# First cross attention of a fused transformer block: maximum's pieces in threes on 32-row tiles, products and banks reordered

## What is computed

```python
qc = x @ w_q + b_q
kc = y @ w_k + b_k
vc = y @ w_v + b_v
scores = jnp.einsum('bhqd,bhkd->bhqk', qh, kh) / math.sqrt(D_HEAD)
attn = jax.nn.softmax(scores, axis=-1)
out = jnp.einsum('bhqk,bhkd->bhqd', attn, vh)
```

## Time and profile before

| | us |
|---|---|
| median of 3 runs | 1087.43 (1084.34 to 1089.31) |
| profiled execution | 1088.43 |
| its span | 1086.5 |

### The profile page before, as it was taken

The page is one execution under the profiler, slowest core; times in us unless marked ns, Lnnn a source line. Parts: engine busy times, 40 slices in busy tenths (PEclk is TensorE's granted clock), DMA queues, the critical chain, the costliest instruction groups (busy, mean ns, idle before and its releaser), DMA issues. The chain is left out here.

```text
span 1086.5 us, 31222 instructions
## 1 busy us (share of the span) xinstructions
PE 999.8 (92%) x11876; PEld 723.2 (67%) x11876; DVE 718.8 (66%) x1369; ACT 560.7 (52%) x1107; POOL 413.5 (38%) x290
## 2 busy tenths in 40 slices
PE   6857989999999999888779999999999999999997
PEld 3633666666666667646327777777777777777786
DVE  6647767677777777212786767767677677767752
ACT  3623767676776666532444454444454453444542
POOL 6513222232222323020106554545556444555542
PEclk9966999999999999989799999999999999999998
DMA  3416565666566652110020112111011111102100
GB/s 126 122 35 161 161 161 157 177 178 174 169 176 166 174 162 72 50 52 1 2 72 28 58 58 60 52 41 56 21 58 56 58 43 49 43 34 58 36 4 3
DMA packets 90924, 91.34 MB, mean 84 GB/s; under 512 B 50882, under 2 KB 77716, under 8 KB 90868
## 3 DMA queue, kind: packets, MB, share of 16 engines
q1 hardware_dynamic: 90868, 90.56, 29.9%
HBM read 51.15 MB, written 22.18 MB: 68 GB/s over the span
## 5 line engine op out<-in xcount | busy, mean ns | idle before, releaser
L1430 ACT ACTIVATE P<-PS 125x448 f32<-125x448 f32 x384 | 207.1, 544 | 265.8 <-PE PS L1339 263.9
L1320 POOL TENSOR_TENSOR Pl<-P 125x896 f16<-125x896 f32 x128 | 229.9, 1801 | 237.7 <-ACT P L1430 237.7
L1066 DVE TENSOR_REDUCE m<-PS 128x1 f32<-128x500 f32 x336 | 220.8, 675 | 115.4 <-PE PS L1057 113.4
L974 DVE TENSOR_REDUCE m_part<-PS 128x1 f32<-128x500 f32 x336 | 208.1, 673 | 86.5 <-PE PS L878 85.2
L1355 PE MATMUL PS<-cNh,P 125*128 125x97 f16 x1344 | 197.9, 208 | 0.1
L952 ACT ACTIVATE Pb<-PS 125x448 f32<-125x448 f32 x384 | 184.2, 546 | 26.5 <-PE PS L853 24.2
L1357 PE MATMUL PS<-cNh,Pl 125*128 125x97 f16 x1344 | 197.4, 207 | 0.0
L1356 PE MATMUL PS<-cNl,P 125*128 125x96 f16 x1344 | 196.8, 206 | 0.0
L1356 PEld LDWEIGHTS PS<-cNl,P 125*128 125x128 bf16 x1344 | 131.8, 98 | 25.5
L878 PE MATMUL PS<-KH,Qmx 128*128 128x500 f16 x336 | 128.0, 391 | 21.3 <-DVE m_part L974 10.8
L1355 PEld LDWEIGHTS PS<-cNh,P 125*128 125x128 bf16 x1344 | 131.1, 98 | 15.7 <-issue 3.2
(11 more groups left out here) (174 smaller groups left out, 1447.8 us busy)
## 6 DMA issues: line engine op xcount, KB each, us to landing
Kst<-k_halves SPq DMA_DIRECT2D x144, 125.0 KB, 2.7
k_halves<-KH SPq DMA_DIRECT2D x16, 750.0 KB, 3.2
cx<-in_ctx SPq DMA_DIRECT2D x16, 562.5 KB
d_cx<-in_ctx SPq DMA_DIRECT2D x16, 562.5 KB
c_halves<-cHi SPq DMA_DIRECT2D x16, 288.0 KB, 2.9
c_halves<-cLo SPq DMA_DIRECT2D x16, 288.0 KB, 6.5
cTh<-c_halves SPq DMA_DIRECT2D x16, 288.0 KB, 3.1
cTl<-c_halves SPq DMA_DIRECT2D x16, 288.0 KB, 3.9
```

The costliest lines, as they stand in the source:

```text
L974: nc.vector.tensor_reduce(m_part[:, t, part:part + 1], PS[:, 6 + k % 2, 0:SP], AX.X, ALU.max).then_inc(s_reduced, 1)
L1066: nc.vector.tensor_reduce(m21[:, t, part:part + 1], PS[:, S1[k % 2], 0:SP], AX.X, ALU.max).then_inc(n_red, 1)
L1320: nc.gpsimd.tensor_tensor(Pl[:, c % NP], P1[:, c % NP], high, ALU.subtract).then_inc(n_low_p, 1)
L1430: nc.scalar.activation(P1[:, c % NP, half * HALF:(half + 1) * HALF], PS[0:KC, u % 3, 0:HALF], ACT.Exp).then_inc(n_exp, 1)
```

## The change

All is in the first cross attention.

- The maximum's pieces: 24 in place of 21, each a matmul with 32 rows (the four heads of group g) and 112 query columns against 500 keys, without the other heads' zero rows. Three of them with three different g are a "three"; they fill banks 5, 6 and 7, and one reduction of 112 x (3 x 500) takes the maximum. There are 8 threes per sequence. A three starts when the reduction of the one before is done.
- Order: threes 1 to 7 at c = 0, 2, 3, 4, 6, 7, 8; three 0 of the following sequence already at c = 13 of the body before. Values' products at c = 0, 1, 2, keys' products at c = 3, 5, 7, `turn_output` at 8, `turn_attention` at 10, and the four small steps (`highest`) at c = 9.
- Banks: the products, the turns and the maximum's turn share one work bank, 3. `turn_output` therefore waits for the third `split_keys`.
- Transposing DMAs of b + 3: issued in the body of b, between the laying of part 1 and of part 2 of the keys, not at the start of the next body.
- The maximum lies in 8 tiles of 112 queries, so on 16 extra rows of Kst and Qst and not 14, with one more block of columns in the table. The second cross attention keeps its 21 pieces under the name NPC1.

Left out of the diff: those sizes in other lines, and lines where only a bank's name changes.

```diff
-        Kst = sb_in(cross, "Kst", [96 + MR, 2, G, SK], F16)
+        Kst = sb_in(cross, "Kst", [96 + MR0, 2, G, SK], F16)
...
-        m_part = sb_in(cross, "m_part", [128, QT, NSP])
-        mtop = sb_in(cross, "mtop", [128, QT])
-        mhigh = sb_in(cross, "mhigh", [128, QT], F16)
-        mneg = sb_in(cross, "mneg", [128, MR])
+        m_part = sb_in(cross, "m_part", [TP, NSP * G, 2])
+        mtop = sb_in(cross, "mtop", [TP, QT0])
+        mhigh = sb_in(cross, "mhigh", [TP, QT0], F16)
+        mneg = sb_in(cross, "mneg", [TP, MR0])
...
-        OB, WB, WB2, MB = 4, 5, 3, 7
-        K_BANK, V_BANK = (WB2, WB, WB2), WB2
-        V_AT = {7: 0, 9: 1, 12: 2}
...
-        PIECES = [(t, part) for part in range(NSP) for t in range(QT)]
-        NPC = len(PIECES)
-        BESIDE = [range(min(2 * c, NPC), min(2 * c + 2, NPC)) for c in range(NC + LAG0)]
+        OB, WB, SB0 = 4, 3, 5
+        V_AT = {0: 0, 1: 1, 2: 2}
...
+        NPC = 2 * NSP * G // 3
+        K_AT = {3: 0, 5: 1, 7: 2}
+        AFTER_SCORES = {2: 2, 3: 3, 6: 5, 7: 6}
+        AT_END = {0: 1, 4: 4, 8: 7}
+        START = {0: 0, 1: 1, 2: 2, 3: 3, 4: 4, 6: 5, 7: 6, 8: 7}
+        NEXT = {13: 0}
...
+        def three(k):
...
+            return k % 2, range(3 * (k // 2), 3 * (k // 2) + 3)
...
-                    if part == 2 and block_row == 1:
+                    if part == 1 and block_row == 1:
...
-                    if part == 2 and block_row == 2 and inside(i, par, 3):
+                    if part == 1 and block_row == 2 and inside(i, par, 3):
...
+                if part == 1 and turn_next:
+                    turn_rows(sp, i, par, 3)
...
-        def work_bank(banks, k, mode):
+        def work_bank(k, mode):
...
-            return (4, 5, 2)[k] if mode == BESIDE_Q else banks[k]
+            return (4, 5, 2)[k] if mode == BESIDE_Q else WB
         def turn_context(pe, i, par, k, mode):
...
             for c in range(4):
-                mm = pe.transpose(PS[0:DC, work_bank(None, k, mode), c * KC:(c + 1) * KC], cx[:, slot, 4 * k + c, :], ident[0:KC, 0:KC])
+                mm = pe.transpose(PS[0:DC, work_bank(k, mode), c * KC:(c + 1) * KC], cx[:, slot, 4 * k + c, :], ident[0:KC, 0:KC])
...
         def k_piece(pe, i, par, k, mode=LOOP):
...
-                pe.wait_ge(v_kept, (n - 1) * 3)
-            elif k == 1:
-                wait_for(pe, att_kept, n - 3)
+                pe.wait_ge(v_kept, n * 3)
...
-                pe.wait_ge(k_split, n * 3 + 1)
-            o = PS[:, work_bank(K_BANK, k, mode), 0:SP].rearrange("p (c k) -> p c k", c=4)
+                pe.wait_ge(k_split, n * 3 + k)
+            o = PS[:, work_bank(k, mode), 0:SP].rearrange("p (c k) -> p c k", c=4)
...
-                if inside(i, par, 2) and not early:
-                    pe.wait_ge(k_split, n * 3 + 6)
+                if not early:
+                    pe.wait_ge(k_split, n * 3 + 3)
...
             for c in range(4):
-                o = PS[0:KC, V_BANK, c * D:(c + 1) * D]
+                o = PS[0:KC, WB, c * D:(c + 1) * D]
...
             def _(sp):
                 def body(i, par):
-                    if inside(i, par, 2) and not (isinstance(i, int) and i < 0):
-                        turn_rows(sp, i, par, 2)
...
-                        lay_keys(sp, i, par, 2)
+                        lay_keys(sp, i, par, 2, turn_next=inside(i, par, 3))
...
-                def score_piece(i, par, k):
...
-                    slot, n = (par + 1) % 2, i * 2 + par + 1
-                    t, part = PIECES[k]
+                def score_three(i, par, k, ahead):
...
+                    slot, n = (par + ahead) % 2, i * 2 + par + ahead
+                    j, where = three(k)
...
-                    if t == 0:
-                        pe.wait_ge(k_high, n * 3 + part + 1)
-                    wait_for(pe, s_reduced, n * NPC + k - 1)
-                    pe.matmul(PS[:, 6 + k % 2, 0:SP], Qmx[:, slot, t * 128:(t + 1) * 128],
-                              KH[:, slot, 0, part * SP:(part + 1) * SP], start=True, stop=True).then_inc(s_filled, 1)
...
-                def turn_output(n, k_before):
+                    if j == 0:
+                        pe.wait_ge(k_high, n * 3 + where[-1] // G + 1)
+                    wait_for(pe, s_reduced, n * NPC + k)
+                    for at, e in enumerate(where):
+                        part, g = e // G, e % G
+                        rows_of = slice(32 * g, 32 * g + 32)
+                        mm = pe.matmul(PS[0:TP, SB0 + at, 0:SP], Qmx[rows_of, slot, (2 * g + j) * TP:(2 * g + j + 1) * TP],
+                                       KH[rows_of, slot, 0, part * SP:(part + 1) * SP], start=True, stop=True)
+                    mm.then_inc(s_filled, 1)
...
+                def turn_output(n, has_2):
...
-                    if k_before is not None:
-                        pe.wait_ge(k_split, k_before)
+                    if has_2:
+                        pe.wait_ge(k_split, n * 3 + 12)
+                    elif n + 2 < B:
+                        pe.wait_ge(v_kept, n * 3 + 9)
...
-                def turn_maximum(i, par):
+                def turn_maximum(i, par, has_b, has_old):
...
+                    if has_old:
+                        pe.wait_ge(att_kept, n - 1)
+                    else:
+                        pe.wait_ge(k_split, n * 3 + 6)
...
-                    pe.matmul(PS[96:96 + MR, MB, 0:128], mneg[:], ident, start=True, stop=True).then_inc(m_turned, 1)
+                    pe.matmul(PS[96:96 + MR0, WB, 0:TP], mneg[:], ident[0:TP, 0:TP], start=True, stop=True).then_inc(m_turned, 1)
                 def body(i, par):
...
                     for c in range(NC + LAG0):
-                        pieces = list(BESIDE[c]) if has_1 else []
...
-                        for k in pieces[:1]:
-                            score_piece(i, par, k)
+                        if has_1 and c == 11:
+                            turn_maximum(i, par, has_b, has_old)
+                        if has_1 and not at_start and c in AFTER_SCORES:
+                            score_three(i, par, AFTER_SCORES[c], 1)
...
-                        if has_2 and 3 <= c < 6:
-                            k_piece(pe, i, par, c - 3)
-                        if has_b and has_old and c == 6:
-                            turn_output(b - 1, b * 3 + 8 if has_2 else None)
...
+                        if has_2 and c in K_AT:
+                            k_piece(pe, i, par, K_AT[c])
...
+                            turn_output(b - 1, has_2)
+                        if has_b and has_old and c == 10:
...
-                        if has_1 and c == 11:
-                            turn_maximum(i, par)
-                        for k in pieces[1:]:
-                            score_piece(i, par, k)
+                        if has_1 and not at_start and c in AT_END:
+                            score_three(i, par, AT_END[c], 1)
+                        if at_start and c in START:
+                            score_three(i, par, START[c], 1)
+                        if has_2 and c in NEXT:
+                            score_three(i, par, NEXT[c], 2)
...
-                turn_output(B - 1, None)
+                turn_output(B - 1, False)
...
-                        if has_2 and 3 <= c < 6:
-                            keep_keys(act, i, par, c - 3)
-                        if has_b and has_old and c == 8:
-                            keep_attention(b - 1)
...
+                        if has_2 and c in K_AT:
+                            keep_keys(act, i, par, K_AT[c])
+                        if has_b and has_old and c == 10:
+                            keep_attention(b - 1)
...
             def _(dve):
-                def reduce_piece(i, par, k):
-                    n = i * 2 + par + 1
+                def reduce_three(i, par, k, ahead):
+                    n = i * 2 + par + ahead
...
-                    t, part = PIECES[k]
-                    nc.vector.tensor_reduce(m_part[:, t, part:part + 1], PS[:, 6 + k % 2, 0:SP], AX.X, ALU.max).then_inc(s_reduced, 1)
+                    j, where = three(k)
+                    nc.vector.tensor_reduce(m_part[:, where[0]:where[-1] + 1, j], PS[0:TP, SB0:SB0 + 3, 0:SP], AX.X, ALU.max).then_inc(s_reduced, 1)
                 def normalise(n):
...
+                def highest(n):
+                    dve.wait_ge(s_reduced, n * NPC + NPC)
+                    nc.vector.tensor_reduce(mtop[:].rearrange("p (g j) -> p g j", j=2), m_part[:].rearrange("p (s g) j -> p g j s", s=NSP), AX.X, ALU.max).then_inc(m_link, 1)
+                    dve.wait_ge(m_link, n * 2 + 1)
+                    nc.vector.tensor_copy(mhigh[:], mtop[:]).then_inc(m_link, 1)
+                    dve.wait_ge(m_link, n * 2 + 2)
+                    wait_for(dve, m_turned, n)
+                    nc.vector.tensor_scalar(mneg[:, 0:QT0], mhigh[:], -1.0, None, ALU.mult)
+                    nc.vector.tensor_tensor(mneg[:, QT0:], mhigh[:], mtop[:], ALU.subtract).then_inc(m_ready, 1)
...
```

(44 more changed lines are left out.)

30 lines of the change are left out of this document (17 added, 13 removed).

## The result

The changed kernel takes 1141.45 us (median of 4 runs, 1139.75 to 1143.34), the kernel before 1087.34 beside it: 1.0492 of it, 95% interval 1.0466 to 1.0518. It is slower by 54 us. Its profiled execution took 1142.51 us with a span of 1140.7.

A forecast was written before the change was run, and what follows sets the result against it. TensorE was taken to set the pace, VectorE next. Fourteen bodies of 25.3 us, a last of 22.0 and 0.4 for half clock gave +36.4, plus 4.1 ahead of the loop: 1128 us, range 1108 to 1160.

The forecast's parts named there:

- the likeliest case: Whole kernel: serial turns of the threes slow it to 1128 us, covering 1109 to 1140; chance 0.67.
- Handover and serial turn: First cross attention: fill, reduction and release of a three run strictly serially, 2.43 us a turn, eight times a body.
- TensorE's price of a three: TensorE's time for three matmuls with changes of tile shape: 0.45 us, with ends of 0.28 and 0.83.
- The rival in which nothing runs together: A three's matmuls don't overlap: 0.83 us in place of 0.45 in seven of eight steps, 1170 us; chance 0.09.
- The body walked in the new order: One loop body stepped from three 0 to the next: 25.3 us for 22.7, TensorE's stalls rising from 2 to 6.
- The clock: Rival: the granted clock falls in the body's stalls, up to 1.5 us a body, 21 in all, 1149 us; chance 0.14.
- Ahead of the loop: Before the first scores: eight serial turns at half clock with three splits between add 4.1 us.
- The transposes: Transposing DMAs in SyncE's queue: issued sooner, they land 1.4 to 3 us before the keys' product needs them.
- this ring: Keys split, keys out, six layings, two transposes, next keys' product; the prediction expected no DMA wait there.
- Faster rival: One reduction over three banks costs far less than three; decides at 1.2 us, 1069 us at 0.86; chance 0.05.
- 2 us times 15: Loop of the kernel before: the most to be had from waits in the first chunks of its fifteen bodies.

The follow-up runs named there:

- filled_few: The changed kernel with 3 and 2 unread fp32 matmuls of 256 columns in its two longest stalls; 1119.4 us, 1.0279 of the kernel before.
- third: The changed kernel with each reduction over 166 of 500 columns, so the maximum covers a third of the scores; 1098.3 us, 1.0096 of the kernel before.
- filled: The changed kernel with 14 and 8 unread fp16 matmuls of 256 columns in its two longest stalls; 1158.9 us, 1.0654 of the kernel before.
- third_both: The changed kernel with reductions over 166 of 500 columns, split of keys 1 behind reduction 5, output's turn at c = 9; 1093.5 us.
- order_only: The kernel before with values' products at c = 0, 1, 2 and sooner transposing DMAs, without the threes; 1074.6 us, 0.9876 of the kernel before.

## Why the prediction came out as it did

The forecast was 1128 us, slower with 0.90, in a range of 1108 to 1160; the time is 1141.5, inside the range and just above the 1109 to 1140 that the likeliest case was to cover. Against the profiled execution of before, +40.4 was summed and +54.1 measured. Step by step:

- **Handover and serial turn: right in kind, too long in size.** Taken 0.65 from a three's start to the reduction, measured 0.47 (297.90 to 298.37); taken 2.43 a turn, measured 2.25. The reduction was taken at 1.71 and is 1.716. TensorE's idle ahead of the threes is 3.0 us a body (28.6 in the 250 us from 150 on), where some 4 were forecast.
- **TensorE's price of a three: too high.** Taken 0.45, measured 291.43 - 291.08 = 0.35. The three matmuls run together (alone they would need 0.65). The Trainium skill's figure ("TensorE: Matmul & The Clock Gate", Part 3: four row tiles of 512 columns at 3.07 times) gave 0.28, as an estimate; the measured 0.35 lies between it and the 0.45 taken. The rival in which nothing runs together is out.
- **The body walked in the new order: right.** 2.0 us of stall ahead of three 6 were forecast and 1.97 measured; 1.3 us ahead of the turn of the output, measured 309.70 less the end of the scores at about 308.53 = 1.17. With the clock held up a steady body is 24.4 (filled_few), forecast 25.3: with 2.25 and 0.35 in place of 2.43 and 0.45 the same walk gives 24.4.
- **The clock: the term that the sum left out.** I gave it 0.14 as a rival, priced at 21 us. It happened, and costs 22.1 (1141.5 less 1119.4); that the two agree is in part luck, since it comes in every second body and costs more there than the 1.5 us taken for each. The argument against it, 2.5 us of work between the two stalls, did not hold: the clock fell at about 281 us, within that work, behind the one stall at 279.43 and before the turn's at 283.34, and stayed at 0.50 to 286.5. In the next body the same stall, at 306.24, did not bring it down; why one does and the next doesn't is open.
- **What is luck in the hit:** the 54 us are 32 at full clock (stalls and the stretch ahead of the loop, less the work saved), where 40 were forecast, and 22 of clock. The likeliest case as I told it, at full clock, isn't what happened, and the time is in the range since one term was too large and one missing. The Trainium skill ("TensorE: Matmul & The Clock Gate", A second HAM failure mode: psum-queue depth-cycling) tells of a kernel whose short idle times between groups of matmuls move the clock up and down. The trace agrees: bodies of 24.9 and 26.4 us alternate.
- **Ahead of the loop:** +4.1 forecast, +6.1 measured (105.24 less 99.12). Of that 2.5 lie ahead of the first three, which starts at 82.08 where the first piece started at 79.60; that much is scatter of single executions: the first reduction starts at 79.4 us in third and at 83.9 in filled, which don't differ ahead of it. The eight turns themselves cost 3.6 (23.16 less 19.52).
- **The transposes: right, with too small a view.** From 150 to 400 us of the changed kernel no wait of TensorE for them is left; the spare was there. But the sum took SyncE's reordering at nothing, "wanted 7 us later". In the changed kernel ScalarE does wait for the context, 2.0 us in all, in 4 of the some 10 bodies of that stretch, and where the threes are made cheap this ring is closed, at 23 us a body.
- **Faster rival:** it was to decide at a reduction of 1.2 us, with 22.6 a body at 1.15. With 0.68 (third) a body is 23.3, slower than before, where the prediction has 21.5 at 0.86. So the walk was wrong below: at most 0.9 us of the gap is clock, and the waits on the single work bank and on SyncE's ring, which the walk had as cover, stand in the traces there. How much each is worth is not shown. A reduction of 0.68 us did not make this change pay, and with the later edits it did not either (third_both, 1.0054).

That values' products first and sooner transposes are by themselves worth 13 us (order_only) was in the prediction only as the 2 us times 15 to be had at most from waits: less than half of it could be had, as other waits took their place. Not tried: units small enough for two sets of banks in turn, and threes with the keys' products at c = 3, 4, 5.

## What to carry to other kernels

Before merging small units behind a semaphore into larger ones, count the handovers that become serial: two banks in turn hide a 0.6 us reduction, while three banks as one unit put its 1.7 us between one fill and the next eight times a body, and TensorE stood idle though it had less work. Stalls of 1 to 2 us cost more than their length where they bring the clock down; a cheap test is to fill them with work nobody reads. A load moved ahead in the DMA queue cost those behind it its traffic here, not its issue.

## What was not expected of the hardware

Three 32x112 matmuls of 500 columns on three row groups took 0.35 us together, against 0.215 for one on the whole array. A 562 KB load issued just ahead of a transposing DMA doubled the time to its landing (4.2 to 8.3 us). And 22 unread matmuls a body in one stage went with 35 us more in a later, unchanged one: its loop, for which the changed kernel brought in no instructions from 760 to 1060 us, then did so 38 times, with waits of up to 5.2 us. Five longer ones in their place did not.
